# A four-layer graph network: features of layers 2 and 3 turned by VectorE and DMA, the norm's scale made for four tiles at once

## The reference

```python
h = jnp.maximum(_layernorm(x, axis=-1), 0.0)     # before each layer
# layer 0: softmax over nodes of (q . (adj @ k)) / sqrt(512), times v
# layer 1: weight = adj * exp(q @ k^T); rows divided by their sum; weight @ v
# layer 2: 8 heads of 64; softmax(q @ k^T * SCALE * 2 adj) @ v, then Wo
# layer 3: Xw = X @ Wv + bv; e = leaky_relu(sj[None, :] + si[:, None] + ab)
#          transition = adj * exp(e) / row sum
#          out = relu(X @ Wk[0] + T X @ Wk[1] + T T X @ Wk[2] + biases)
x = x + layer(h)
```

## Time and profile before

| what | value |
|---|---|
| median of 3 runs | 2557.31 us (2555.6 to 2558.02) |
| profiled execution | 2557.38 us, its span 2555.6 us |
| PE busy | 2487.7 us, 97% of the span |
| PEld busy | 2043.4 us, 80% |
| DVE busy | 1261.1 us, 49% |
| POOL busy | 886.0 us, 35% |
| ACT busy | 822.4 us, 32% |
| DMA, 16 engines | 15.2% |
| granted PE clock, mean | 0.99 |

### The profile page before, as it was taken

One profiled execution on the slowest core, in us unless ns is written; L12 is line 12 of the kernel. 1 busy time (PEld: TensorE's weight loads), 2 busy tenths in 40 slices (PEclk: granted clock), 3 DMA queues, 4 the chain that ended last, 5 costly groups with the idle time before them and its releaser, 6 DMA issues.

```text
span 2555.6 us, 41069 instructions
## 1 busy us (share of the span) xinstructions
PE 2487.7 (97%) x17119; PEld 2043.4 (80%) x17119; DVE 1261.1 (49%) x2508; ACT 822.4 (32%) x1493; POOL 886.0 (35%) x1248
## 2 busy tenths in 40 slices
PE   8999999999999998999999999999879999999999
PEld 5788888888888877888888888888667878788877
DVE  2455455454554554333443344434655656556563
ACT  3333333333333333333333333333323232323231
POOL 3444454444454433322342234322441222212120
PEclk9999999999999998999999999999889999999999
DMA  4011111111111121111121111111311111112110
GB/s 145 22 38 38 52 61 38 38 38 38 38 38 56 52 100 54 38 38 38 39 74 38 38 39 56 57 38 46 134 48 38 55 51 54 52 43 64 39 51 33
DMA packets 102904, 130.86 MB, mean 51 GB/s; under 512 B 45552, under 2 KB 45632, under 8 KB 102720
## 3 DMA queue, kind: packets, MB, share of 16 engines
q1 hardware_dynamic: 102720, 128.25, 15.2%
HBM read 77.90 MB, written 50.33 MB: 50 GB/s over the span
## 4 chain that ended last, share of the span: by engine, by line
PE 82%; DVE 6%; POOL 6%; issue 2%; ACT 2%; DMA 1%; SPq 0%; ACTq 0%; POOLq 0%; DVEq 0%
PE bank L305 38%; PE bank L295 27%; PE bank L285 3%; PE bank L611 3%; PE bank L321 2%; POOL stA L1233 2%; PE bank L372 2%; POOL stA L1231 2%; PE bank L530 1%; PE bank L503 1%; DVE yt L942 1%; PE bank L274 1%; PE bank L513 1%; DVE rst L913 1%; DVE yt L957 1%
## 5 line engine op out<-in xcount | busy, mean ns | idle before, releaser
L305 PE MATMUL bank<-w_hi,h3T_hi 128*128 128x512 f32 x768 | 306.1, 399 | 17.1 <-DVE Z_lo L643 17.1
L305 PE MATMUL bank<-w_lo,h3T_hi 128*128 128x512 f32 x768 | 300.3, 391 | 0.0
L305 PE MATMUL bank<-w_hi,h3T_lo 128*128 128x512 f32 x768 | 300.1, 391 | 0.0
L1308 POOL TENSOR_TENSOR zt<-zt,sm 128x512 f32<-128x512 f32 x64 | 66.3, 1046 | 516.6 <-DVE sm L831 516.6
L982 ACT ACTIVATE hn<-x,stA 128x512 f32<-128x512 f32 x192 | 151.5, 812 | 259.7 <-POOL stA L1233 259.7
L305 PEld LDWEIGHTS bank<-w_hi,h3T_hi 128*128 128x128 f32 x768 | 144.8, 189 | 49.6 <-DVE Z_lo L643 20.5
L305 PEld LDWEIGHTS bank<-w_hi,h3T_lo 128*128 128x128 f32 x768 | 144.7, 188 | 30.8
L305 PEld LDWEIGHTS bank<-w_lo,h3T_hi 128*128 128x128 f32 x768 | 144.8, 189 | 29.4
L643 DVE TENSOR_TENSOR cT_lo<-bank,cT_hi 128x256 fp32r<-128x256 f32 x128 | 45.3, 416 | 224.9 <-ACT cT_hi L968 224.9
L643 DVE TENSOR_TENSOR Z_lo<-bank,Z_hi 128x512 fp32r<-128x512 f32 x128 | 84.2, 687 | 143.2 <-ACT Z_hi L968 143.1
L1281 POOL TENSOR_TENSOR vv_lo<-vf,vv_hi 128x512 fp32r<-128x512 f32 x64 | 82.5, 1289 | 206.9 <-ACT vv_hi L968 206.9
(11 more groups left out here) (248 smaller groups left out, 6470.3 us busy)
## 6 DMA issues: line engine op xcount, KB each, us to landing
mid<-x SPq DMA_DIRECT2D x32, 1024.0 KB, 4.6
x<-mid SPq DMA_DIRECT2D x32, 1024.0 KB, 5.7
x<-in_x SPq DMA_DIRECT2D x16, 1024.0 KB, 5.5
out<-x SPq DMA_DIRECT2D x16, 1024.0 KB, 4.5
abf<-in_adj SPq DMA_DIRECT2D x64, 64.0 KB, 4.6
adj<-in_adj SPq DMA_DIRECT2D x64, 64.0 KB, 4.6
w_raw<-in_L_gnn_Wk SPq DMA_DIRECT2D x3, 1024.0 KB, 8.8
wqk<-in_L_gnn_Wqk SPq DMA_DIRECT2D x2, 1024.0 KB, 6.3
```

Of the source, the lines that this page charges most:

```text
L305: ins = eng.matmul(b[:], h[l][:, k, ts], W[r][:, k, :], start=(k == 0 and i == 0), stop=(last and k == 3 and i == 2))
```

## The change

In layers 2 and 3 TensorE no longer transposes features, and PSUM no longer holds them.
- `norm` writes the clipped tile (Relu for Identity) in these layers.
- VectorE transposes hn in 32x32 blocks, one instruction a tile (`transposes`), into `hs`: within each quarter of 32 partitions a block is turned, but it stays in its quarter.
- SP copies the blocks to the quarter where they belong with 16 DMAs a group (`gather`), each of 32 partitions by 2048 bytes, from `hs` into `hG`.
- ScalarE copies hG into hi (`features2_hi`). VectorE writes lo in layer 2 (`features2_lo`), GpSimd in layer 3 (`features3_lo`); both read two tensors of SBUF.
- `scale` takes four tiles at once (norm A) or three and then one (norm B), with four steps instead of three a tile.
- Statistics, scale and norm of the next group stand earlier in layer 2, and so do the loads of x; in layer 3 `l3_sums` is cut in two, around the second half of the Z_lo.

```diff
+            def transposes(layer, g, ts):
+                k = kT(layer, g)
+                for q in range(4):
+                    dve.wait_ge(d_h[q], 64 * k)
+                for t in ts:
+                    dve.wait_ge(a_nA, 4 * kA(layer, g) + t + 1)
+                    eng.transpose(hs[:, :, :, t, :].rearrange("p b c r -> p c b r"),
+                                  hn[t][:].rearrange("p (c b r) -> p c b r", c=4, b=4)).then_inc(v_tr, 1)
+
+            def features2_lo(g):
+                h = hT2[g % 2]
+                for q in range(4):
+                    dve.wait_ge(a_fhi[2], 4 * g + q + 1)
+                    lo_split(by_token(h["lo"], q), hG[:, q], by_token(h["hi"], q)).then_inc(v_flo[2], 1)
...
+                if g + 1 < NG:
+                    stats_A(2, g + 1)
...
                 if prev:
                     l2_out(g - 1, 0)
+                if g + 1 < NG:
+                    transposes(2, g + 1, range(4))
+                if prev:
                     l2_ctx(g - 1, 1)
...
                 if g + 1 < NG:
                     stats_A(3, g + 1)
-                    l3_sums(dve, eng, g + 1)
                 for t in range(4):
                     l3_zlo(0, ("z2", g, t), g, t)
+                    if t == 1 and g + 1 < NG:
+                        transposes(3, g + 1, range(4))
+                        l3_sums(dve, eng, g + 1, (0, 1))
                     if g == 0 and t == 2:
                         l3_rowsum(0)
                 if g + 1 < NG:
-                    features_lo(3, g + 1, hT3[(g + 1) % 2])
+                    l3_sums(dve, eng, g + 1, (2, 3))
...
+            def features2_hi(layer, g, h):
+                for q in range(4):
+                    act.wait_ge(d_h[q], 64 * (kT(layer, g) + 1))
+                    copy(by_token(h["hi"], q), hG[:, q]).then_inc(a_fhi[layer], 1)
...
-            def scale(st, stats, done, n, t):
-                s = st[t]
+            def scale(st, stats, done, n, t0, t1):
+                mean, var, eps, inv, off = (st[:, t0:t1, i] for i in range(6, 11))
                 pool.wait_ge(stats, n)
-                m = pool.step(eng.tensor_scalar(s[:, 8:9], s[:, 7:8], EPS, None, ALU.add))
+                pool.step(eng.tensor_scalar(off, mean, -1.0, None, ALU.mult))
+                m = pool.step(eng.tensor_scalar(eps, var, EPS, None, ALU.add))
                 pool.wait_ge(s_pool, m)
-                m = pool.step(eng.tensor_tensor(s[:, 9:10], s[:, 8:9], mhalf[:], ALU.pow))
+                m = pool.step(eng.tensor_tensor(inv, eps, mhalf.to_broadcast([128, t1 - t0]), ALU.pow))
                 pool.wait_ge(s_pool, m)
-                eng.tensor_scalar(s[:, 10:11], s[:, 6:7], s[:, 9:10], -1.0, ALU.mult, ALU.mult).then_inc(done, 1)
+                eng.tensor_tensor(off, off, inv, ALU.mult).then_inc(done, 1)
...
+            def features3_lo(g):
+                h = hT3[g % 2]
+                for q in range(4):
+                    pool.wait_ge(a_fhi[3], 4 * g + q + 1)
+                    eng.tensor_tensor(by_token(h["lo"], q), hG[:, q], by_token(h["hi"], q).bitcast(F), ALU.subtract).then_inc(p_flo3, 1)
...
                 if on0:
-                    for t in range(3):
-                        scale(stB, v_stB, p_stB, 4 * g + t + 1, t)
+                    scale(stB, v_stB, p_stB, 4 * g + 3, 0, 3)
...
+            def gather(layer, g):
...
+                sp.wait_ge(v_tr, 4 * k + 4)
+                for q in range(4):
+                    for b in range(4):
+                        eng.dma_start(hG[b * 32:b * 32 + 32, q].rearrange("p c r -> p (c r)"),
+                                      hs[q * 32:q * 32 + 32, b].rearrange("p c t r -> p (c t r)")).then_inc(d_h[q], 16)
...
                 if prev:
-                    load2(g + 1)
                     load_adj2(g + 1)
...
+                gather(2, g + 1)
...
             for g in range(NG):
                 load3(g + 2)
+                gather(3, g + 1)
```

More of the change, by code:

```diff
@@ L142, in build @@
         onesr = alloc(root, "onesr", [128, 2], R)
[L143 to L148, removed]
+        small = alloc(root, "small", [128, 4])
+        mhalf, cst, abc, s0 = (small[:, i:i + 1] for i in range(4))
+        stA, stB = alloc(root, "stA", [128, 4, 12]), alloc(root, "stB", [128, 4, 12])
+        late = stB[:].rearrange("p t n -> p (t n)")
+        bqk, af = late[:, 0:8], late[:, 8:16].rearrange("p (k h) -> p k h", h=2)
+        scol = [late[:, 16 + 8 * i:24 + 8 * i].rearrange("p (t c) -> p t c", c=2) for i in range(2)]
         xs = [alloc(root, f"x{i}", [128, 4, 512]) for i in range(3)]
@@ L161, in build @@
         Wa1, Wv1 = pair(pa, "a1"), pair(pa, "v1")
-        ucol, s0 = alloc(pa, "ucol", [128, 4]), alloc(pa, "s0", [128, 1])
+        cols = alloc(pa, "colst", [128, 16])
+        ucol, wS, pcol, rcol = (cols[:, i:i + 4] for i in range(0, 16, 4))
         bv1, crow = alloc(pa, "bv1", [128, 512]), alloc(pa, "crow", [128, 512])
@@ L343, in l01_wt @@
                 pe.wait_ge(v_ws, g + 1)
-                eng.transpose(b[0:4, 0:128], wS[:], ident[:]).then_inc(full, 1)
+                eng.transpose(b[0:4, 0:128], wS, ident[:]).then_inc(full, 1)
             def l01_pt(g):
@@ L472, in pe_program @@
                 else:
-                    features(2, 0, hn, a_nA, 4 * kA(2, 0))
                     l01_sums(g - 1)
@@ L794, in dve_program @@
                         features_lo(0, g + 1, hT[0])
+                    else:
+                        transposes(2, 0, range(4))
                     dve.wait_ge(v_x1, 4 * g + 4)
@@ L867, in dve_program @@
                         l2_softmax(g, u)
-                    if u == 0 and g + 1 < NG:
-                        stats_A(2, g + 1)
+                    if u == 0 and g == NG - 1:
+                        stats_A(3, 0)
                 if g == NG - 1:
+                    transposes(3, 0, range(4))
                     m = dve.step(eng.tensor_tensor(sc3[:], awb[:, 0, :], awb[:, 1, :], ALU.add))
                     dve.wait_ge(s_dve, m)
-                    m = dve.step(eng.scalar_tensor_tensor(sc3[:], sc3[:], 1.0, bvb[:], ALU.mult, ALU.mult, accum_out=cst[:]))
+                    m = dve.step(eng.scalar_tensor_tensor(sc3[:], sc3[:], 1.0, bvb[:], ALU.mult, ALU.mult, accum_out=cst))
                     dve.wait_ge(s_dve, m)
-                    eng.tensor_tensor(cst[:], cst[:], abc[:], ALU.add).then_inc(v_cst, 1)
-                    stats_A(3, 0)
+                    eng.tensor_tensor(cst, cst, abc, ALU.add).then_inc(v_cst, 1)
                 if on:
@@ L946, in dve_program, with l3_sums @@
                         l3_rowsum(g + 1)
-        def l3_sums(dve, eng, g):
+        def l3_sums(dve, eng, g, ts):
             dve.wait_ge(v_arow, 2)
             dve.wait_ge(p_sib, g - 1)
-            for t in range(4):
+            for t in ts:
                 dve.wait_ge(a_nA, 4 * kA(3, g) + t + 1)
@@ L1038, in norm_B @@
                         act.wait_ge(v_dot, 4 * (g - 1) + t + 1)
-                    norm(hn1, stB, p_stB, 4 * g + t + 1, a_nB, xs[x_slot(kA(0, g))], t)
-            for half, dst in enumerate((qT, kT)):
+                    norm(hn1, stB, p_stB, 2 * g + 1 + t // 3, a_nB, xs[x_slot(kA(0, g))], t)
+            for half, dst in enumerate((qT, kTw)):
                 for cc in range(4):
@@ L1482, in sp_program @@
                 if g == NG:
+                    gather(2, 0)
                     load2(1)
```

162 lines of the change are left out of this document (89 added, 73 removed).

## The result

The changed kernel takes 2679.27 us (median of 4 runs, 2675.0 to 2682.53), the kernel before 2557.66 us beside it: ratio 1.0476, 95% interval 1.0458 to 1.0494, slower by 121.6 us. The forecast was 2652 with a range of 2580 to 2700: the sign, the largest term and its mechanism were right, the sum was 27 us short. The profiled execution spans 2678.1 us, with a mean granted clock of 0.961.

What follows compares the result with a forecast made beforehand. TensorE, busy 97% of the span, was taken as the bound between layer seams. Terms 86 - 10 + 13 + 6 + 0 = +95 us on 2557.4 gave 2652 us, range 2580 to 2700 for 8 in 10.

Steps and rivals of the forecast that it cites:

- Layer 3, +86: Layer 3, groups 1 to 14: 6.8 us wait for sib plus 2.4 clock less 3.05 saved each, +86 us.
- the period without them is 40.26: Layer 3: a group's period without the feature transposes and the late Z_lo wait, 40.26 us against 43.31.
- The stall without the clock: Layer 3 rival: TensorE waits 6.8 us a group but returns at full speed; 2618 us, chance 0.13.
- Transposes at half rate: Rival in layers 2 and 3: block transposes take 1.24 us each, so TensorE waits longer; 2715 us, chance 0.10.
- Faster: Layer 3 rival: the arow sums come in time and its 3.05 us a group are gained; 2523 us, chance 0.10.
- A late gather: Rival: gather lands 4 us late in layer 2, costing at most 1.5 us a group; 2673 us, chance 0.04.
- Layer 2, -10 for 14 periods: Layer 2: 1.75 us a group saved, 0.8 to 1.0 given back as h2T_lo meets GpSimd's bias add; -10 us.
- Layers 0 and 1, +13: Layers 0 and 1: norm B's batched scale delays h0T_lo and tile 3's norm, 0.85 us in 15 groups, +13 us.
- The wider power step: Layers 0 and 1: unknown cost of the batched scale's power step, making that term 0 to +24 us.
- Seam 1 to 2, +6: Layer 1 to 2: late adj loads delay softmax, h2T_lo and q2 by 4.5 us, plus 1.5 of clock; +6 us.
- 5.4 us later: Start of layer 2: first adj loads queue on SP behind the transposes' wait and 16 DMAs, 5.4 us later.
- Seam 2 to 3, 0: Layer 2 to 3: next si 1.6 us earlier, less 2.4 of clock; 0 us, range -15 to +10.

Runs made afterwards that it cites:

- the sums first: Changed kernel with VectorE's layer 3 order put back: all arow sums and scol ahead of Z_lo and block transposes; 2612.30 us, ratio 1.0216.
- the doubled transposes: Changed kernel with each of layer 3's four block transposes made twice, from group 1 on; 2720.57 us, ratio 1.0638.

## Why the prediction was right, and where it was short

- **Layer 3, +86: measured +88.4.** Every station came within 0.6 us of its forecast. The terms of a group are now 7.05 (wait; forecast 6.8) + 2.55 (clock and restart; 2.4) - 3.28 (what is saved, 43.21 - 39.93; 3.05). So "the period without them is 40.26" was nearly right, and the small errors partly cancel, which is luck. Off most was the batched scale, 1.96 us instead of 1.45 (its power step takes 1.04 us for four columns, 0.57 for one). The transpose, the price that no row of before showed, is 0.62 us (four in 2.48), the value taken. The Trainium skill (Vector Engine (DVE) Microarchitecture Reference, section 3.8) has one element per cycle and lane, an estimated 0.53 us before overhead; the trace agrees with that. That the wait is set by VectorE's order was argued then and is shown now, by the sums first, and from the other side by the doubled transposes. (The prediction's S + 18.3 for TensorE at `si` before reads S + 18.1 in its trace; nothing rests on it.)
- **Rivals.** "The stall without the clock" fell with the windows above and 2.04 against 1.06 us for the same matmuls. "Transposes at half rate" fell with 0.62. "Faster" needed scol at S+13.7, and it came at S+20.7. A late gather cost nothing in layer 2's steady groups; in layer 3 it is hidden behind the `si` wait, and shows only once that is gone.
- **Layer 2, -10 for 14 periods: -11.9 for 13.** The collision of h2T_lo with the bias add is there and costs 0.88 us a group, which moving the add gave back; the forecast had 0.8 to 1.0.
- **Layers 0 and 1, +13: measured +25.1.** This step was mis-sized, and just beyond its upper end of +24. The place was right (waits for h0T_lo and hnB, 0.57 and 0.38 us a group in the trace, where the forecast had 0.4 and 0.45). The wider power step, named as the unknown, took 0.88 us for three columns and made the scale end 0.25 us later than priced. The larger part of the miss is another: the period grew by 1.54 us and the two waits are only 0.95 of it. The other 0.6 is lost in TensorE's matmuls behind them (its weight loads stand idle for 1.0 and 0.6 us at the same two places), and the sum had no term for that, though it had one in layer 3 (0.1 us of restart). Undoing the batch gave 20.7 back.
- **Seam 1 to 2, +6: measured +13.3.** The step that failed is "5.4 us later" for the adj loads. The forecast knew an issue by the 0.4 us of a 1 MB load; the 16 took 0.63 us each with the gap, 11 us in all, and the loads came 11.5 us late against the first q2 matmul of their group. The trace of before had a nearer row, SyncE's issues of the eight adj loads, 64 KB each like those of the gather, at 0.78 us each:

```profile
999.86 6.25 SPq L1443 DMA_DIRECT2D adj<-in_adj  x8
```

  With adj first, 10.7 us of the first period came back. Another 4.1 of the 13.3 us lie ahead of the first q2 matmul (102.0 us from the last g0, 97.9 before). The forecast had nothing there, and moving the transposes won 1.0 back; the rest stays open.
- **Seam 2 to 3, 0: measured +5.8.** The forecast named the collision of the sums with h3T_lo and W1's split, and had other gains balance it. All eight took 1.6 us instead of 0.69 (before, only the last two), and `sib` made TensorE wait 8.2 us. 2.2 us of the 5.8 stand ahead of the first `si`. The other 3.6 stand behind it, where the first hop waits 16.7 us for Tlo; the kernel before had 12.9 us of waits there, for the norms of group 1 and Z_lo.

## What to carry to other kernels

Work taken off the busiest engine must be priced by the engine that takes it over, at the place in its program where it lands: four transposes and the order around them left a period of 49.5 us, and two altered orders took 9.0 us a group off it, so that the same transposes ended 2.7 us below the kernel before. Queue many small transfers behind what is needed soonest, and count their issues by their own price. Batching tiny instructions pays only if nobody waits for the first result; here it cost 21 us in one place and 0.6 us a group in another, and gave 2.4 us once, because GpSimd's next work started sooner.

## What the runs showed that I had not expected

- GpSimd's power step grows with the columns: 0.57, 0.88 and 1.04 us for 1, 3 and 4 columns of 128 partitions, while its other small steps stay at 0.2 to 0.3; beside VectorE's sums, which read two SBUF tensors, three of them took 1.24 to 1.30 us in layer 3 of the kernel before. Four tiles at once take 1.96 us, four single ones in three steps each 5.2 (before, layer 2), but the first of the single ones is out after 1.24.
- A two-SBUF instruction of VectorE can stand for the whole of one GpSimd instruction: the longest h2T_lo took 5.08 us beside the bias add's 5.05, its median 0.69.
- SyncE's issue of a 64 KB transfer of 32 partitions (0.59 us and a gap) costs more than that of a 1 MB one of 128 partitions (0.37).
